# Making the attention's one-hots of local nodes on ScalarE instead of storing and loading them

## The reference, cut to what matters

```python
h7  = segment_sum(xw[col] * norm[:, None], row)          # layer 0: sums over edges, then an MLP
out = segment_sum(h[row] * norm[:, None], col)           # layer 1: sums over edges
for l in range(3):                                       # layer 2: typed attention, three times
    scores = sum(Q[dst] * kt, -1) / scale * mu[l].T[edge_type]
    e = exp(scores - segment_max(scores, dst)[dst])
    agg = segment_sum(V[src] * (e / s[dst])[..., None], dst)
out = segment_sum(h_src * attn[..., None], dst)          # layer 3: attention with edge attributes
```

## Time and profile before

| | |
|---|---|
| median of 3 runs | 5548.44 us (5533.56 to 5564.57) |
| profiled execution, its own time | 5535.18 us |
| its span | 5533.5 us |
| busy in the span: PE | 4208.4 us (76%) |
| busy: DVE | 3814.4 us (69%) |
| busy: POOL | 3333.5 us (60%) |
| busy: ACT | 1622.2 us (29%) |
| mean granted TensorE clock | 0.905 |
| moved by DMA | 959.77 MB, mean 173 GB/s |

### The profile page before, as it was taken

One profiled execution on the slowest core, in us unless ns is written; L12 is line 12 of the kernel. 1 busy time (PEld: TensorE's weight loads), 2 busy tenths in 40 slices (PEclk: granted clock), 3 DMA queues, 4 the chain that ended last, 5 costly groups with the idle time before them and its releaser, 6 DMA issues. The chain is left out here.

```text
span 5533.5 us, 69081 instructions
## 1 busy us (share of the span) xinstructions
PE 4208.4 (76%) x19341; PEld 3323.8 (60%) x19341; DVE 3814.4 (69%) x8692; ACT 1622.2 (29%) x3882; POOL 3333.5 (60%) x3108
## 2 busy tenths in 40 slices
PE   4666666377777678887987888798788878878886
PEld 4554445254444566666886666688666667756665
DVE  6644444275555569998436999853699986679998
ACT  3443334230000432222443222234322223422221
POOL 2388888717777467774136777513677750067775
PEclk9888888689999889998998999999899999989998
DMA  4488888736666577786027787612787762077775
GB/s 159 102 123 124 124 122 124 112 118 209 211 212 210 169 236 240 238 242 190 23 73 235 241 244 238 199 32 73 224 245 237 238 188 67 17 220 235 233 239 171
DMA packets 525140, 959.77 MB, mean 173 GB/s; under 512 B 87701, under 2 KB 299875, under 8 KB 523954
## 3 DMA queue, kind: packets, MB, share of 16 engines
q0 software_dynamic: 224512, 549.90, 39.6%
q1 hardware_dynamic: 300130, 404.93, 22.9%
q10 hardware_dynamic: 128, 0.52, 0.0%
HBM read 718.56 MB, written 236.50 MB: 173 GB/s over the span
## 5 line engine op out<-in xcount | busy, mean ns | idle before, releaser
L1462 POOL DMA_INDIRECT L2a_rows<-kv_rows,typed_index x960 | 957.8, 998 | 292.5 <-issue 292.5
L1767 PE MATMUL L2a_sums<-L2a_weighted,L2a_hot 128*128 128x264 f32 x2784 | 791.1, 430 | 204.6 <-DVE L2a_weighted L1617 174.5
L867 POOL DMA_INDIRECT sum_rows<-L0s_rows,L0s_row_of x464 | 726.8, 1566 | 153.7 <-issue 119.3
L1756 PE MATMUL L2a_query<-x,L2a_turned 128*128 x2784 | 727.9, 408 | 50.5 <-ACT L2a_turned L1711 27.8
L1767 PEld LDWEIGHTS L2a_sums<-L2a_weighted,L2a_hot 128*128 128x128 f32 x2784 | 555.3, 209 | 347.8 <-DVE L2a_weighted L1617 199.1
L1756 PEld LDWEIGHTS L2a_query<-x,L2a_turned 128*128 128x128 f32 x2784 | 568.4, 207 | 152.5 <-issue 56.5
L1286 POOL DMA_INDIRECT L1s_rows<-rows,index x464 | 451.1, 972 | 270.4 <-ACTq L87 129.2
L1462 POOL DMA_INDIRECT L3a_rows<-feature_rows,index x464 | 480.9, 1037 | 154.9 <-issue 154.9
L1002 PE MATMUL L0s_message<-features,L0s_share 128*128 x928 | 314.9, 498 | 292.4 <-ACT L0s_share L967 292.4
L1462 POOL DMA_INDIRECT hold<-kv_rows,typed_index x432 | 429.0, 993 | 178.4 <-issue 178.4
L2298 POOL TENSOR_SCALAR L2d_here<-hold,mask 128x256 f32<-128x256 f32 x200 | 183.1, 934 | 537.8 <-DVE hold L2374 389.7
(11 more groups left out here) (428 smaller groups left out, 8319.0 us busy)
## 6 DMA issues: line engine op xcount, KB each, us to landing
code_rows<-L1s_code SPq DMA_DIRECT2D x232, 256.0 KB, 2.9
L3a_code<-code_rows SPq DMA_DIRECT2D x116, 512.0 KB, 4.0
L0s_wide<-source_rows SPq DMA_DIRECT2D x116, 256.0 KB, 3.9
L2a_turn<-turned_rows SPq DMA_DIRECT2D x87, 256.0 KB, 4.4
L2a_pens<-mask_rows SPq DMA_DIRECT2D x87, 256.0 KB
L2a_hot<-hot_rows SPq DMA_DIRECT2D x87, 256.0 KB, 3.9
kv_rows<-L2d_key_rows SPq DMA_DIRECT2D x50, 384.0 KB, 2.6
kv_rows<-L2d_value_rows SPq DMA_DIRECT2D x150, 128.0 KB, 2.4
```

What stands on the lines that cost most here:

```text
L867: pool.indirect_dma_start(c.sum_rows[u], bass.IndirectOffsetOnAxis(ap=row_of[:, 4 * n + u:4 * n + u + 1], axis=0), rows[n % ring][:, u, :] ...
L1462: pool.indirect_dma_start(rows[n % ring][:, u, :], None, table, bass.IndirectOffsetOnAxis(ap=index_of[:, t:t + 1], axis=0)).then_inc(lande ...
L1756: last = pe.matmul(query[q % 2][:, u, :], turned[quad % 2][:, u, :], at(c.q, b[2 * q + u // 2]), start=True, stop=True)
L1767: last = pe.matmul(sums[(m * WP + j) % held][:, :], hot[quad % 2][:, j % 2 * 2 + k, :], weighted[:, 2 * j + k, :], start=k == 0, stop=k == 1)
```

## The change

ScalarE makes the float32 one-hots in the attention stages from `c.count` and `c.local`: for each of a quad's four tiles the absolute value of local minus count, then over the whole quad relu(1 - that), which is 1 where the two are equal and 0 elsewhere. Between the two ACT waits for its own result (semaphore `away_ready`), and the 1 comes from a new constant `c.one`. The bytes `hot8` go in both stages, with ACT's packing, SP's stores and loads, the memory `hot_rows` and their semaphores; DVE's `mark` of the first sums waits for PE alone.

```diff
@@ constants
+            pool.memset(c.one[:, :], 1.0)
@@ spread_sum, SP
-                sp.wait_ge(packed, n + 1)
-                sp.dma_start(c.hot_rows[:, own], hot8[n % 2][:, :]).then_inc(hot_stored[n % 2], 16)
@@ spread_sum, DVE, mark
                 wait(dve, mixed_ready, n - hots + 1)
-                wait(dve, packed, n - hots + 1)
@@ spread_sum, ACT
                 if n:
                     deliver(n - 1)
-                if n >= 2:
-                    act.wait_ge(hot_stored[n % 2], 16 * (n // 2))
-                act.wait_ge(hot_ready, n + 1)
-                act.activation(hot8[n % 2][:, :], hot[n % hots][:, :, :].rearrange("p u n -> p (u n)"), ACT.Copy
-                               ).then_inc(packed, 1)
@@ attend, SP
-            def load_hot(n):
-                wait(sp, hot_ready, (n - 1) * WQ)
-                sp.dma_start(hot8[n % 2][:, :], c.hot_rows[:, n * WT * P:(n + 1) * WT * P]
-                             ).then_inc(hot_landed[n % 2], 16)
...
                 load_pens(n)
-                load_hot(n)
@@ attend, ACT (widen is now mark, at the same five places of the order)
-            def widen(m, q):
+            def mark(m, q):
                 quad = m * WQ + q
                 if 0 <= m < WG:
-                    wait(act, hot_landed[m % 2], 16 * (m // 2 + 1))
                     wait(act, sums_ready, (quad - 1) * 2)
-                    act.activation(hot[quad % 2][:, :, :].rearrange("p u e -> p (u e)"),
-                                   hot8[m % 2][:, q * 4 * P:(q + 1) * 4 * P], ACT.Copy).then_inc(hot_ready, 1)
+                    for u in range(4):
+                        t = 4 * quad + u
+                        last = act.activation(hot[quad % 2][:, u, :], c.count[:, :], ACT.Abs, scale=-1.0,
+                                              bias=c.local[:, t:t + 1])
+                    last.then_inc(away_ready, 1)
+                    wait(act, away_ready, quad + 1)
+                    flat = hot[quad % 2][:, :, :].rearrange("p u e -> p (u e)")
+                    act.activation(flat, flat, ACT.Relu, scale=-1.0, bias=c.one[:, :]).then_inc(hot_ready, 1)
```

More of the change, by code:

```diff
@@ L836, in spread_sum @@
         wide = [st.sb(f"wide{s}", [P, 4, P]) for s in range(wides)]
-        hot8 = [st.sb(f"hot8_{s}", [P, 4 * P], U8) for s in range(2)]
         turn8 = [st.sb(f"turn8_{s}", [P, 4 * P], U8) for s in range(2)]
@@ L846, in spread_sum @@
                                 "moved", "row_ready", "counted"))
-        mixed_ready, taken, turned, packed, message_ready, delivered = (
-            st.sem(x) for x in ("mixed_ready", "taken", "turned", "packed", "message_ready", "delivered"))
+        mixed_ready, taken, turned, message_ready, delivered = (
+            st.sem(x) for x in ("mixed_ready", "taken", "turned", "message_ready", "delivered"))
         added = [st.sem(f"added{k}") for k in range(KT)]
-        hot_stored, turn_stored = ([st.sem(f"{x}{s}") for s in range(2)] for x in ("hot_stored", "turn_stored"))
+        turn_stored = [st.sem(f"turn_stored{s}") for s in range(2)]
         wide_landed = [st.sem(f"wide_landed{s}") for s in range(wides)]
@@ L892, in _ @@
             for s in range(2):
-                for stored in (hot_stored, turn_stored):
-                    sp.wait_ge(stored[s], 16 * (quads // 2))
+                sp.wait_ge(turn_stored[s], 16 * (quads // 2))
         @block.vector
@@ L1414, in attend @@
         turn8 = [st.sb(f"turn8_{k}", [P, WT * P], U8) for k in range(2)]
-        hot8 = [st.sb(f"hot8_{k}", [P, WT * P], U8) for k in range(2)]
         pens = [st.sb(f"pens{k}", [P, 4, P]) for k in range(2)]
@@ L1440, in attend @@
         landed = [st.sem(f"landed{s}") for s in range(ring)]
-        turn_landed, hot_landed, pens_landed = (
-            [st.sem(f"{x}_landed{k}") for k in range(2)] for x in ("turn", "hot", "pens"))
-        (turned_ready, hot_ready, query_ready, multiplied, score_ready, flat_ready, scanned, ends_ready, seq_ready,
+        turn_landed, pens_landed = ([st.sem(f"{x}_landed{k}") for k in range(2)] for x in ("turn", "pens"))
+        (turned_ready, away_ready, hot_ready, query_ready, multiplied, score_ready, flat_ready, scanned, ends_ready, seq_ready,
          chained, gap_ready, fall_ready, tops_ready, picked, reached, zz_ready, diag_ready, below_ready, shrink_ready,
@@ L1446, in attend @@
             st.sem(x) for x in (
-                "turned_ready", "hot_ready", "query_ready", "multiplied", "score_ready", "flat_ready", "scanned",
+                "turned_ready", "away_ready", "hot_ready", "query_ready", "multiplied", "score_ready", "flat_ready", "scanned",
                 "ends_ready", "seq_ready", "chained", "gap_ready", "fall_ready", "tops_ready", "picked", "reached",
@@ L1737, in _ @@
                 m = n - 1
-                widen(m, 1)
+                mark(m, 1)
                 turn(n + 1, 0)
@@ L1742, in _ @@
                 soften(m)
-                widen(m, 2)
+                mark(m, 2)
                 turn(n + 1, 2)
-                widen(m, 3)
+                mark(m, 3)
                 turn(n + 1, 3)
-                widen(n, 0)
+                mark(n, 0)
         @block.tensor
@@ L3050, in program @@
         c.typed_index = sb("typed_index", [P, NT], I32)
+        c.one = sb("one", [P, 1])
         c.each, c.head, c.heads = sb("each", [P, WT]), sb("head", [P, H]), sb("heads", [H, P])
@@ L3062, in program @@
         c.field_rows = nc.dram_tensor("field_rows", [4, NT, P], F32, kind="Internal").ap()
-        c.hot_rows = nc.dram_tensor("hot_rows", [P, NT * P], U8, kind="Internal").ap()
         c.code_rows = nc.dram_tensor("code_rows", [P, NT, D], F32, kind="Internal").ap()
```

## The result

The changed kernel takes 5561.65 us (median of 19 runs, 5552.7 to 5575.57), the one before 5549.4 us (19 runs, 5532.13 to 5571.05). The ratio is 1.0026 with a 95% interval of 1.0016 to 1.0035, so 14.4 us more (8.9 to 19.4); the two medians differ by 12.3. That is "within 0.5%" and inside the forecast range, but not zero: the sum had 1.1 us, and the question of this study is where the other 13 come from.

The account below looks back on a forecast made before the run. POOL's gathers, scatters and their issue were taken as the bound: 5535.18 us profiled plus 1.0 for stage ends and 0.1 for a constant made 5536.3, or 5549 us on the median's scale, range 5518 to 5585.

Parts of the forecast that it names:

- What sets the pace: First sums and attention: POOL is busy or issuing from first tile to last; 880, 605 and 636 us a stage.
- bytes were the bound: Rival, first sums and attention: dropped stores and loads save 62 and 132 us, giving 5355 us; chance 0.05.
- The first sums at 0: First sums: dropping ACT's packing pays 0, and DVE's moved one-hots cost scatters 0, between -7 and 51 us.
- one-hots on scatters: Rival, first sums: DVE's moved one-hots stretch POOL's scatters by 0.44 us a quad, up to 5600 us; chance 0.09.
- ACT's price: Attention: a one-hot quad takes ACT 1.96 us instead of 0.63, 617 us more busy time, steady state costing 0.
- The condition of the lower bound: ACT's four Abs per quad: 1.0 us at least, if input from SBUF saves 0.035 us each.
- The cover that the drop had in ordinary windows: Ordinary attention windows: ACT's drop still ends 0.47 us before DVE's step needs it, so dearer one-hots cost 0.
- the rival's second condition: Rival of ACT holding up DVE, attention: lateness must also exceed DVE's spare 1.5 us per window; 5616 us, chance 0.04.
- The ends of the stages at 1.0 us: Last window of four attention stages: third and fourth one-hot quads delay an add by 0.25 us each, 1.0 us together.
- The price that moves: POOL's gathers stretched by DVE's weighings: 113 us in attention left unchanged, 10 us to either side.
- Weighings for the better: Rival, attention: rows land sooner and a third of the 113 us of gather stretching goes, 5511 us; chance 0.05.
- The reading of the 2.00 us row: Attention: a gather beside DVE's weighing took 2.00 us, taken to contradict the skill's rule that descriptor writing isn't held up.

Follow-up runs that it names:

- loads_gone: Kernel before, conversions kept, one-hot bytes loaded only for the first two windows of each attention stage and reused: 5548.64 us, ratio 1.0011.
- pack_kept: Changed kernel with the first sums' packing and stores of one-hot bytes put back, nothing loading them: 5554.87 us, ratio 1.0024 to the kernel before.
- abs_twice: Changed kernel with four more Abs per one-hot quad, written into a spare tile: 5601.28 us, ratio 1.0101 to the kernel before.
- loads_kept: Changed kernel that also packs, stores, loads and waits for the one-hot bytes without using them: 5541.99 us, ratio 0.9989 to the kernel before.
- before_again: Kernel before, unchanged, profiled once more to see how far single profiles scatter: 5536.27 us.
- hot4: Changed kernel with four one-hot buffers instead of two in the attention stages: 5551.65 us, ratio 1.0012 to the kernel before.
- loads_kept_hot4: Changed kernel with four one-hot buffers and the bytes packed, stored and loaded but unused: 5542.27 us, ratio 0.9999 to the kernel before.
- before_prob_small: Kernel before, with probabilities also written to a free PSUM corner for the weighing to read, and the fourth weighing moved earlier: 5474.43 us, ratio 0.9868.

## Why the prediction was right, and what it mis-sized

**What sets the pace: right.** POOL waits for no DMA in attention, before or after. (Of the 154.9 us ahead of L3a's gathers some 14 lie before the first one; its stage before is 622 us, not 636, which no term of the sum uses.) The rival "bytes were the bound" (5355 us) falls with loads_gone: the loads' bytes are gone and the kernel is no faster. The Trainium skill ("SBUF — State Buffer", section A bandwidth-pool intuition that's wrong) has HBM as almost always the bottleneck; here it isn't, 38 MB less moved and 14 us more.

**The first sums at 0: right**, by pack_kept and the scatters' means. DVE's wait went from ACT's packing to ACT's counts (435.3 us), as forecast; the rival "one-hots on scatters" (5600 us) did not occur.

**ACT's price: right.** 2.03 us a quad for a forecast of 1.96, busy time 2169.8 for 2170, no wait in ordinary windows. Its parts are off and partly cancel: the four Abs take 1.28 us for 1.14, and the wait for ACT's own result 0.03 for 0.1. The condition of the lower bound, that input from SBUF saves 0.035 us each, went the other way: they are 0.035 us each above the row. The cover that the drop had in ordinary windows was real (the drop still ends 0.42 us or more ahead of DVE's step), and thin: with 1.28 us more a quad, abs_twice uses it up in 83 windows of L2a. But the rival's second condition, DVE's spare of 1.5 us a window, was the wrong test: lag that POOL never sees is still paid where the stage ends.

**The ends of the stages at 1.0 us: too small.** The term measured about 8 us from timelines, and 6.1 as the mean of all profiles (109.9 us for after, pack_kept and loads_kept; 103.8 for before, before_again, loads_gone, hot4 and loads_kept_hot4). The step costed the third and fourth quads only, at 0.25 us. In the last window the drop stands behind a quad too, and the cover that I had read from an ordinary window isn't there, since DVE has no next window's work between its steps: it reaches the step 1.37 us after the quad's start, where the earlier trace rows have 3.24. In hot4's timelines this term is gone; its total, 1.0012 after 1.0026, agrees, within intervals that overlap.

**The price that moves, left at 0: the wrong step.** "In attention DVE's order and its releasers are not edited" overlooked that the landing of rows releases DVE too. Without the loads, DVE's second product starts about 0.6 us sooner after its gather, its fourth product runs into rows that have not landed three times as often, and gathers start during the third weighing. That is 11.1 us in L2a, and it goes with the loads, not with ACT's edit: loads_gone has it without that edit, loads_kept is rid of it with it. By the runs' own times the loads are worth 6 us (before to loads_gone), 19 (pack_kept to loads_kept) and 7 (hot4 to loads_kept_hot4). The bounds given for it, 10 us to either side, were 1 us too narrow. "Weighings for the better" named the right mechanism; the sign was the other one. The sum is now 11.1 + 6.1 = 17.2 us, where 14.4 (8.9 to 19.4) were measured. That the forecast held nonetheless is owed to its range, which allowed 14 us for stretching and scatter, and not to these two terms.

**The reading of the 2.00 us row.** It is the two operands in SBUF: the product, with one in PSUM, stretches nothing, and moving one operand of the weighing to PSUM takes the stretching away in three kernels. The Trainium skill ("SBUF — State Buffer", section Who interferes with whom) says that a two-SBUF-input tensor_tensor holds up a GpSimd instruction that reads SBUF; I counted the gather as descriptor writing and the row as speaking against the page. The runs agree with that half of the rule, if the gather reads the row numbers in its SBUF tile `typed_index`, which no run here shows by itself.

**Open.** By the term that stays, loads_kept should be some 6 us above the kernel before (1.0011), and it is 6 us below (0.9989); its three L2a stages are 7 us under the mean of their group in its one profile, for which I have no reason. Four buffers on top don't make it faster (0.9999; the intervals overlap). L3a's gathers don't follow the loads (1030 to 1047 ns in both groups). Over all gathers of L2a the median from issue to landing is 3.9 us with loads and 3.8 without; the later landing shows in the second quad's rows, and how the load brings it about (a shared queue, the memory or else) was not told apart.

## What to carry to other kernels

An engine that waits for data has a phase, and traffic sets it: before a transfer is removed as free, look at what its absence lets run earlier and what that will collide with. A deep ring hides the lag of everything behind the pacing engine until the stage runs dry, so cost an edit on the last window of a stage, whose neighbours in each queue are missing, as well as on one in the middle. And where one engine's mean lies above its median, find out what stretches it before optimizing anything else: here that was worth 1.3%, and the change under study cost 0.3%.

## What the runs showed of the hardware that was not expected

- A GpSimd gather that starts during a DVE tensor_tensor with two SBUF operands ends about 0.8 us after that instruction does: 2115.07 less 2114.25 = 0.82 us, and 2477.40 less 2476.59 = 0.81 us in loads_gone. In the timeline of before, of 428 gathers that start during a weighing 416 last more than 0.05 us above the median, and these end 0.81 to 0.84 us after the weighing; of 438 that start during a product, which has the weighing's size and one operand in PSUM, none lasts more than 0.02 us above it. With one operand of the weighing in PSUM a gather takes its 0.95 us, and the means of gathers fall from 998 and 1037 ns to 949 and 950 (before_prob_small).
- ACT waiting for its own last result through a semaphore is idle for 0.03 us (11.3 us over 348 quads); without a wait its next activation starts 0.10 us before the last one ends.
- Abs, Relu, Copy and Exp take turns in every window of attention without a function table being loaded in between: the softening line has four table loads after as before, one a stage.
